# Moving the next batch's group norm and projections out of the head of a batch and in between the expert tiles of the batch before

## The chip, the cores and the metric

The kernel runs on one core of a Trainium2 chip. The metric is device time in microseconds (us) for one execution of the whole program. An engine is named by its short name: PE is TensorE (matrix products), ACT is ScalarE, DVE is VectorE, POOL is GpSimd, SP is the queue of SyncE that issues DMAs. PEld is PE's loading of weights, which runs beside its products.

## What is computed

Four images of 64 x 64 positions with 128 channels go through two layers. All is float32.

```
# layer 0, per batch: N = 4096 tokens, 4 heads of 32
xn  = group_norm(x)                       # 32 groups of 4 channels
q, k, v = split(xn @ w_qkv)
q, k = q / |q|, k / |k|                   # norm along the tokens, per channel
x = x + softmax(10 * q k^T) v @ w_out + b_out
# layer 1, linear attention
z = layer_norm(x);  q, k, v = split(W_qkv z)
q = softmax(q, over a head's 32 channels) * 32**-0.5;  k = softmax(k, over the tokens)
context = k v^T (per head);  y = W_out (context q) + b
x = x + norm_over_everything(y) * gn_w + gn_b
# layer 1, experts
z = layer_norm(x);  p = softmax(z @ router_w + router_b)
x = x + sum over the best 2 of 8 experts of weight * (z @ expert_w[e] + expert_b[e])
```

## The kernel before

The batches run one after the other (`for b in range(batches)` on each engine). The instructions of every engine are written out in program order by hand, and engines meet at semaphores (`wait_ge`, `then_inc`). No scheduler moves anything. PSUM is used as eight banks `BK[0]` to `BK[7]` of 128 x 512 float32. A "chunk" is 512 tokens (8 in a batch, `NCH`), a "tile" 128 tokens (32 in a batch, `T`).

A batch has four stages, given here with the times of the second change of batch in the trace (batch 1 to batch 2), which the prediction follows:

- **The head of a batch** (1540 to 1572 us). After the last expert tile DVE ends the group norm's factor (`s_gn`). PE transposes the batch's x, which waits in `XN` (L1127, 32 transpositions). DVE and ACT write it, scaled and shifted, into `XT` by turns. PE makes keys and queries from it (8 chunks each, `projected`) and then values (32 tiles of 128 tokens). DVE and ACT evict them and take the sums of squares and the maximum of the squares of q. DVE turns these into deviations and a flag (`s_bound`, `s_flag`), scales `Q`, and attention can start.
- **Attention** (1572 to 2117 us): 8 chunks of 32 tiles. PE makes scores, ACT exponentials, PE the products with `V`, DVE adds the exponentials up in `ACC`, which shares its memory with `XT`. SP loads the next batch's x into `XN` in this stage, and DVE takes its group statistics between the adds. At its end `projected_first` on PE multiplies chunks 0 to 6 by `WOUT0`.
- **Linear attention** (1359 to 1453 us for batch 1). DVE adds onto `X` (L915) and takes a layer norm in two halves. PE transposes z into `XT`, makes keys (`s_k1`), then values of layer 1 (`token_major(..., s_v1)`), which ACT evicts into `V` (`values1`, L577), then queries. ACT takes the exponentials of the keys (L599), PE transposes them and sums `K^T V` into `BK[0]`, DVE makes `CTX` and `AT` out of it.
- **Experts** (1464 to 1540 us). For each of the 32 tiles PE makes the products with all 8 experts into two banks (`expert_bank`, three such pairs, `EBUF = 3`; PE may be three tiles ahead). DVE multiplies four of them by the gates and adds them to `X` (L1091), ACT scales the other four (L636), POOL adds those up. `biases` and `gates` are small products of PE that come every four tiles and twice. DVE has the routing of both halves to do ahead of and between its first tiles.

The two places that matter for order: PE waits for `s_comb` and `s_zx` of the tile three before it ahead of every expert tile, and at the top of a batch for those of all tiles.

## Time and profile before

| | |
|---|---|
| median of 3 runs | 3062.41 us (3049.99 to 3062.47) |
| the profiled execution | 3062.7 us, its span 3060.9 us |
| PE busy | 2890.6 us, 94% of the span |
| DVE, ACT, POOL busy | 84%, 79%, 23% |
| mean granted clock of TensorE | 0.974 |
| attention, one chunk | 67.8 us, 8 chunks a batch |
| one batch to the next | 757.7 us |

The shares are means over stages with different limits. Time of the profiled execution outside its span is 1.8 us. A stage is read from the chain that ended last and from the timeline of its engines. Matmul records are counted as two where a float32 product takes two passes; a transposition has one.

### The profile page before, as it was taken

How to read it: one execution, taken by the hardware profiler on the slowest of the kernel's cores; microseconds unless marked ns; L12 is line 12 of the kernel's file. 1: busy time of each engine (PE TensorE's matmuls, PEld its weight loads, DVE VectorE, ACT ScalarE, POOL GpSimd, SP SyncE). 2: the span in 40 equal slices, each digit the busy share in tenths (PEclk: the TensorE clock that was granted, in tenths of full speed). 3: DMA queues.
4: the chain of work that ended last, by engine and by line, in shares of the span. 5: the costliest groups of instructions: out<-in, count | busy, mean ns of one | idle time of the engine just before them, and what ended most of it. 6: DMA issues, size and time to landing. Idle time of an engine off the chain costs nothing.

```text
span 3060.9 us, 52576 instructions
## 1 busy us (share of the span) xinstructions
PE 2890.6 (94%) x20414; PEld 1024.5 (33%) x20414; DVE 2576.4 (84%) x3687; ACT 2415.2 (79%) x3141; POOL 712.6 (23%) x726
## 2 busy tenths in 40 slices
PE   6999999989899999998989999999898999999988
PEld 3222222275422222237532222223743222222474
DVE  6888888878788888986878888898687888888867
ACT  5999999753799999974479999997447999999734
POOL 1122222113312222111432222121152222121115
PEclk9999999998999999999899999999899999999989
DMA  2655555500265555550026555554002555555300
GB/s 88 115 111 111 109 113 111 98 1 14 59 121 109 111 112 111 97 97 1 21 66 116 113 112 111 99 111 84 1 21 56 112 112 113 101 109 110 73 1 28
DMA packets 72081, 257.03 MB, mean 84 GB/s; under 512 B 8160, under 2 KB 10240, under 8 KB 71808
## 3 DMA queue, kind: packets, MB, share of 16 engines
q0 software_dynamic: 64512, 234.91, 40.6%
q1 hardware_dynamic: 7296, 18.51, 1.6%
q8 instruction: 168, 2.75, 0.4%
q14 instruction: 105, 0.86, 0.1%
HBM read 10.12 MB, written 8.39 MB: 6 GB/s over the span
## 4 chain that ended last, share of the span: by engine, by line
PE 84%; DVE 8%; ACT 5%; issue 2%; POOL 1%; DMA 0%; SPq 0%; POOLq 0%; DVEq 0%; ACTq 0%
PE BK L1122 81%; PE BK L1127 3%; DVE X L1091 2%; ACT EA L548 2%; ACT KE L548 2%; DVE MXS L941 1%; DVE ST L668 1%; ACT K L599 1%; POOL KE L473 1%; ACT SMC L537 0%; DVE KE L700 0%; DVE XT L824 0%; DVE RU L662 0%; DVE RU L661 0%; PE BK L1424 0%
## 5 line engine op out<-in xcount | busy, mean ns | idle before, releaser
L877 DVE TENSOR_TENSOR XT<-XT,KE 128x512 f32<-128x512 f32 x1344 | 1572.7, 1226 | 148.8 <-ACT KE L548 146.4
L548 ACT ACTIVATE KE<-BK 128x512 f32<-128x512 f32 (+1 forms) x1536 | 1490.5, 1022 | 129.9 <-PE BK L1122 34.5
L1122 PE MATMUL BK<-Q,K 32*128 32x512 f32 x8192 | 1167.8, 640 | 18.5 <-ACT KE L548 12.2
L1122 PE MATMUL BK<-KE,V 128*32 128x512 f32 x6144 | 815.0, 604 | 5.3 <-ACT SMC L537 5.3
L432 POOL DMA_DIRECT2D RM<-EA x448 | 393.3, 959 | 1506.9 <-ACT EA L548 650.3
L1122 PEld LDWEIGHTS BK<-Q,K 32*128 32x128 f32 x8192 | 319.9, 183 | 874.8 <-ACT KE L548 626.6
L548 ACT ACTIVATE EA<-BK 128x512 f32<-128x512 f32 (+1 forms) x512 | 497.5, 1025 | 26.6
L1122 PEld LDWEIGHTS BK<-KE,V 128*32 128x32 f32 x6144 | 125.3, 108 | 582.7 <-issue 533.0
L1122 PE MATMUL BK<-EA,V 128*32 128x512 f32 x2048 | 272.6, 604 | 0.0
L636 ACT ACTIVATE RM<-BK,GT 128x128 f32<-128x128 f32 x512 | 146.3, 368 | 139.6 <-PE BK L1122 139.6
L1122 PE MATMUL BK<-WEXP,XT 128*128 128x512 f32 x512 | 243.0, 621 | 14.0 <-DVE X L1091 14.0
L1091 DVE SCALAR_TENSOR_TENSOR X<-BK,GT,X 128x128 f32<-128x128 f32 x512 | 175.1, 350 | 32.5 <-PE BK L1122 16.3
L851 DVE TENSOR_TENSOR XT<-KE 128x512 f32<-128x512 f32 x64 | 88.8, 1393 | 124.2 <-ACT KE L548 124.2
L482 POOL TENSOR_TENSOR Z<-RM 128x512 f32<-128x512 f32 x64 | 81.2, 1269 | 272.2 <-ACT RM L636 272.2
L1122 PEld LDWEIGHTS BK<-WEXP,XT 128*128 128x128 f32 x512 | 98.1, 201 | 124.3 <-issue 93.5
L413 POOL TENSOR_TENSOR Q<-PVC,REC 128x512 f32<-128x512 f32 x32 | 70.1, 2189 | 250.5 <-DMA RM<-EA 125.4
L1122 PEld LDWEIGHTS BK<-EA,V 128*32 128x32 f32 x2048 | 40.7, 108 | 193.5 <-issue 171.1
L831 DVE RECIPROCAL REC<-SMC 128x512 f32<-128x512 f32 x28 | 93.6, 3342 | 0.0
L1122 PE MATMUL BK<-WQKV,XT 128*128 128x128 f32 x768 | 89.4, 276 | 0.0
L1122 PEld LDWEIGHTS BK<-WQKV,XT 128*128 128x128 f32 x768 | 87.9, 192 | 4.0 <-issue 3.8
L1122 PE MATMUL BK<-XT,WQKV 128*128 128x512 f32 x192 | 86.5, 604 | 0.0
L824 DVE TENSOR_TENSOR XT<-XT,RM 128x512 f32<-128x512 f32 x64 | 75.3, 1217 | 0.2 <-POOLq L440 0.2
(182 smaller groups left out, 1849.3 us busy)
## 6 DMA issues: line engine op xcount, KB each, us to landing
RM<-EA POOLq DMA_DIRECT2D x224, 768.0 KB, 6.7
RM<-EA POOLq DMA_DIRECT2D x224, 256.0 KB, 3.3
XN<-in_x SPq DMA_DIRECT2D x16, 512.0 KB, 6.2
out<-X SPq DMA_DIRECT2D x16, 512.0 KB, 2.6
WEXP<-in_L_ffn_expert_w SPq DMA_DIRECT2D x1, 512.0 KB, 6.6
CONST<-in_consts SPq DMA_DIRECT2D x1, 384.0 KB, 5.4
WQKV<-in_L_conv_w_qkv SPq DMA_DIRECT2D x1, 192.0 KB, 2.2
WQKV<-in_L_attn_W_qkv SPq DMA_DIRECT2D x1, 192.0 KB, 5.8
```

What stands on the lines that cost most here:

```text
L413: nc.gpsimd.tensor_tensor(Q[:, c * CH:(c + 1) * CH], PVC[:, :], REC[:, :], ALU.mult).then_inc(s_ot, 1)
L432: nc.gpsimd.dma_start(DACC[:, PART[p]], EA[:, k % 2, PART[p]], accum_op=ALU.add).then_inc(s_dacc[p], 16)
L482: nc.gpsimd.tensor_tensor(Z2[:, :, :], z[:, :, 0:2 * C], z[:, :, 2 * C:4 * C], ALU.add).then_inc(s_zs, 1)
L548: nc.scalar.activation(exps(jt, p), scored(c * T + jt, p).rearrange("p a n -> p (a n)"), ACT.Exp, scale=SCALE0).then_inc(s_exp, 1)
L636: last = nc.scalar.activation(ZX[:, t // 2 % 2, t % 2, k], expert_bank(t, 1)[:, k], ACT.Copy, scale=GT[:, t, e:e + 1])
L824: v.tensor_tensor(acc, acc, DACC[:, PART[p]], ALU.add).then_inc(s_merge, 1)
L831: v.reciprocal(REC[:, :], row_sums).then_inc(s_rec, 1)
L851: v.tensor_tensor(ACC[:, par, PART[p]], exps(0, p), exps(2, p), ALU.add).then_inc(s_adds, 1)
L877: v.tensor_tensor(acc, acc, exps(jt, p), ALU.add).then_inc(s_adds, 1)
L1091: v.scalar_tensor_tensor(X[:, t, :], expert_bank(t, 0)[:, e * C:(e + 1) * C], GT[:, t, e:e + 1], X[:, t, :], ALU.mult, ALU.add).then_inc(s ...
L1122: return nc.tensor.matmul(o, lhsT, rhs, start=start, stop=stop, skip_group_check=shared)
L1127: last = nc.tensor.transpose(dst[:, (t % TPB) * P:(t % TPB + 1) * P], src(t), IDENT)
```

## The change

What it does:

- `V` is free between attention and the next batch's attention, since layer 1 has no values of its own any more: PE sums `K^T z` (`Z` holds z as tokens) and multiplies the 128 x 128 result by the value weights once (`KZ`, `s_kz`). `values1`, its 32 records on PE for each half and its 8 evictions on ACT are gone.
- After the last products of attention, PE transposes the next batch's x (`turned_following`, 32 transpositions into banks 4, 5 and 6 by turns), and ACT copies it raw into `V` (`VT`, `s_raw`). The `WOUT0` products of chunks 4 to 6 go behind the first half's transpositions of z.
- The group norm's two small products and its chain of DVE operations go to the middle of layer 1 (`group_means`, `group_moments`, `group_spread`, `group_norm`), and ACT normalises `VT` in place in two lots of four chunks (`normalise`).
- The 24 projections of the next batch (8 keys, 8 queries, 8 chunks of values) stand behind 24 of the 32 expert tiles (`project_following`, all but every fourth tile), in banks 5 and 6. ACT evicts them alone (`evicted`), with the squares. Expert tiles have two pairs of banks (three in the last batch).
- DVE takes the maxima of q's squares after the tiles of chunks 5 and 6, the deviations ahead of chunk 7, the flag among chunk 7's tiles.
- Batch 0 has its head as before.

On PE, the expert stage of batch 0. `BK<-WEXP,XT` is an expert tile (two instructions), `BK<-EB,GTT` the biases, `G` and `GTT` the gates, `V` the next batch's x. Before, from the first expert tile:

```order
L1122 MATMUL BK<-WEXP,XT 128x512 x2
L1424 MATMUL BK<-CONST,G 128x128 x4
L1122 MATMUL BK<-WEXP,XT 128x512 x2
L1122 MATMUL BK<-EB,GTT 128x128 x4
L1122 MATMUL BK<-WEXP,XT 128x512 x4
L1122 MATMUL BK<-EB,GTT 128x128 x4
L1122 MATMUL BK<-WEXP,XT 128x512 x8
```

In the changed kernel, from the same place:

```order
L1218 MATMUL BK<-WEXP,XT 128x512 x2
L1552 MATMUL BK<-CONST,G 128x128 x4
L1218 MATMUL BK<-WEXP,XT 128x512 x2
L1218 MATMUL BK<-V,WQKV 128x512
L1218 MATMUL BK<-EB,GTT 128x128 x4
L1218 MATMUL BK<-WEXP,XT 128x512 x2
L1218 MATMUL BK<-V,WQKV 128x512
L1218 MATMUL BK<-WEXP,XT 128x512 x2
L1218 MATMUL BK<-V,WQKV 128x512
L1218 MATMUL BK<-EB,GTT 128x128 x4
L1218 MATMUL BK<-WEXP,XT 128x512 x4
L1218 MATMUL BK<-V,WQKV 128x512
```

A projection now stands behind three of each four tiles, so PE is nowhere idle by order, and the transpositions and products of the head of the next batch are gone.

On DVE, the end of the same stage. `X<-BK8,GT,X` is a gated add of one expert, `MXS` the maxima, `Q` the queries. Before:

```order
L1083 TENSOR_TENSOR X<-BK8,X 128x512
L1091 SCALAR_TENSOR_TENSOR X<-BK8,GT,X 128x128 x16
L1083 TENSOR_TENSOR X<-BK8,X 128x512
L1091 SCALAR_TENSOR_TENSOR X<-BK8,GT,X 128x128 x16
```

In the changed kernel, from the maxima after chunk 6 on (the chain for the deviations is 15 rows, of which the first and last stand here):

```order
L805 TENSOR_REDUCE MXS<-KE 128x1 x4
L810 TENSOR_REDUCE RA<-MXS 128x1
...
L816 TENSOR_TENSOR SMALL<-SMALL,RA 128x1
L828 TENSOR_SCALAR Q<-Q,SMALL 128x512
L1160 TENSOR_TENSOR X<-BK8,X 128x512
L1171 SCALAR_TENSOR_TENSOR X<-BK8,GT,X 128x128 x8
L821 TENSOR_REDUCE SMALL<-BK8 1x1
```

Between the last add of tile 27 and the first of tile 28 DVE now has four maxima, the chain and one scaling.

On PE, behind attention. `WOUT0,Q` are the output products of layer 0, `XT,CONST` the sums of the last chunk, `XN` the next batch's x, `KE` z, `WQKV1` the weights of layer 1. Before:

```order
L1122 MATMUL BK8<-WOUT0,Q 128x128 x16
L1122 MATMUL BK8<-XT,CONST 32x512 x4
L1122 MATMUL BK8<-WOUT0,Q 128x128 x12
L1300 UNCONDITIONAL_BRANCH
L1127 MATMUL BK8<-CONST,KE 128x128 x16
L1122 MATMUL BK8<-XT,WQKV1 128x512 x4
L1122 MATMUL BK8<-WOUT0,Q 128x128 x4
L1122 MATMUL BK8<-WQKV1,XT 128x128 x32
```

In the changed kernel:

```order
L1218 MATMUL BK8<-WOUT0,Q 128x128 x16
L1223 MATMUL BK8<-CONST,XN 128x128 x8
L1218 MATMUL BK8<-XT,CONST 32x512 x4
L1223 MATMUL BK8<-CONST,XN 128x128 x24
L1416 UNCONDITIONAL_BRANCH
L1223 MATMUL BK8<-CONST,KE 128x128 x16
L1218 MATMUL BK8<-WOUT0,Q 128x128 x12
L1218 MATMUL BK8<-XT,WQKV1 128x512 x4
L1218 MATMUL BK8<-WOUT0,Q 128x128 x4
L1218 MATMUL BK8<-WQKV1,XT 128x128 x16
```

The transpositions of x took the place of twelve `WOUT0` products, which moved behind z's transpositions, ahead of the keys and of chunk 7's `WOUT0` products; 16 products of layer 1's values are gone.

The diff, cut to its core:

```diff
 def group_bank(b):
-            return BK[0] if b else BK[NCH - 1]
+            return BK[5] if b else BK[NCH - 1]
+        def expert_buffers(b):
+            return 2 if b + 1 < batches else 3
+        def projection_of(t):
+            return t - 1 - t // TPB if t % TPB else None
+        def projection_bank(j):
+            return BK[5 + j % 2]
+        def turned_bank(i):
+            return BK[HCH + i % 3]
...
# ACT, behind attention
+                if b + 1 < batches:
+                    for i in range(NCH):
+                        act.wait_ge(s_xT, (b + 1) * NCH + i + 1)
+                        nc.scalar.activation(VT[:, i * CH:(i + 1) * CH], turned_bank(i), ACT.Copy).then_inc(s_raw, 1)
...
# ACT, layer 1 and experts
-                for c in range(HCH, NCH):
-                    values1(c)
...
+                def normalise(chunks):
+                    act.wait_ge(s_gn, b + 2)
+                    for c in chunks:
+                        xt = VT[:, c * CH:(c + 1) * CH]
+                        nc.scalar.activation(xt, xt, ACT.Identity, bias=SMALL[:, 4:5], scale=SMALL[:, 3:4]).then_inc(s_xn, 1)
+                def evicted(j):
+                    c, columns = j % NCH, slice(j % NCH * CH, (j % NCH + 1) * CH)
+                    act.wait_ge(s_proj, (b + 1) * (3 * NCH) + j + 1)
+                    if j < NCH:
+                        nc.scalar.activation(SQ[:, 0, columns], projection_bank(j), ACT.Square, accum_out=SS[:, 0, c:c + 1])
+                        nc.scalar.activation(K[:, columns], projection_bank(j), ACT.Copy).then_inc(s_kev, 1)
...
+                    if following and t and projection_of(t - 1) is not None:
+                        evicted(projection_of(t - 1))
...
# DVE
+                dve.wait_ge(s_ctx, b * 3 + 1)
+                v.tensor_copy(KZ[:, :], BK[0][:, 0:C]).then_inc(s_kz, 1)
+                dve.wait_ge(s_ctx, b * 3 + 2)
+                v.scalar_tensor_tensor(CTX[:, :], BK[0][:, C:2 * C], SMALL[:, 11:12], BLOCK,
                                        ALU.mult, ALU.mult).then_inc(s_at, 1)
...
+                if following:
+                    pre_link, pre_n = chain(s_pre, (b + 1) * PRE_LINKS)
+                    group_spread(b + 1)
+                    group_norm(b + 1, pre_link)
...
# PE, experts
+                def project_following(j):
+                    m, c = j // NCH, j % NCH
+                    if j >= 2:
+                        before = j - 2
+                        signal = (s_kev, s_qev, s_v)[before // NCH]
+                        pe.wait_ge(signal, (b + (signal is s_v)) * NCH + before % NCH + 1)
+                    if m == 0:
+                        pe.wait_ge(s_xn, b * NCH + c + 1)
...
+                    if following and t == T - 2:
+                        pe.wait_ge(s_bound, b + 2)
                         pe.wait_ge(s_eba, b * NCH + HCH)
+                        mm(bound_bank(b + 1)[0:1, 0:H], SMALL[:, 14:15], BLOCK[:, 0:P:D]).then_inc(s_gm, 1)
+                    if t >= buffers:
+                        pe.wait_ge(s_comb, b * COMB + (t - buffers + 1) * NDVE)
+                        pe.wait_ge(s_zx, b * T + t - buffers + 1)
...
+                    if following and projection_of(t) is not None:
+                        project_following(projection_of(t))
```

## Rows read from the trace of the kernel before

**Rows 1.** The page: busy time of an engine; chain's shares.

```profile
PE 2890.6 (94%) x20414; PEld 1024.5 (33%) x20414; DVE 2576.4 (84%) x3687; ACT 2415.2 (79%) x3141; POOL 712.6 (23%) x726
...
PE 84%; DVE 8%; ACT 5%; issue 2%; POOL 1%; DMA 0%; SPq 0%; POOLq 0%; DVEq 0%; ACTq 0%
```

**Rows 2.** The chain that ended last, whole program: start, length, work.

```profile
1396.51 4.08 ACT K L599 x4
...
1544.08 5.19 PE BK L1127 x32
```

**Rows 3.** Timeline of PE, last expert tiles and first scores: start, length, work, [idle before].

```profile
1531.65 7.11 PE L1122 MATMUL BK<-WEXP,XT 128*128 128x512 f32 x16
...
1572.18 1.14 PE L1122 MATMUL BK<-Q,K 32*128 32x512 f32 x8 [0.78 <-ACT V L519]
```

**Rows 4.** Groups by line and shape, 1540.3 to 1572.2 us: busy, mean ns.

```profile
L1122 PE MATMUL BK<-XT,WQKV 128*128 128x512 f32 x32 | 13.9, 592 | 0.0
L1122 PE MATMUL BK<-WQKV,XT 128*128 128x128 f32 x64 | 7.6, 277 | 0.0
```

**Rows 5.** Timeline of PE in the expert stage.

```profile
1473.60 1.98 PE L1122 MATMUL BK<-WEXP,XT 128*128 128x512 f32 x4 [0.61 <-DVE X L1091]
...
1499.78 1.12 PE L1424 MATMUL BK<-CONST,G 128*128 128x128 f32 x4 [2.64 <-DVE GT L1072]
1500.68 6.37 PE L1122 MATMUL BK<-WEXP,XT 128*128 128x512 f32 x12
...
1507.79 7.03 PE L1122 MATMUL BK<-WEXP,XT 128*128 128x512 f32 x16
```

**Rows 6.** Windows: length, busy of PE, PEld, DVE, ACT, POOL; clock, DMA, GB/s.

```profile
1463.90:1538.80 74.90, 68.73 (x207) 34.51 (x207) 61.88 (x178) 35.63 (x125) 40.28 (x44) 0.95 0.05 22
1373.00:1377.00 4.00, 4.00 (x18) 3.69 (x19) 4.00 (x5) 4.00 (x10) 0.00 (x0) 0.57 0.00 0
1545.00:1549.00 4.00, 4.00 (x29) 4.00 (x28) 2.56 (x4) 2.12 (x3) 0.00 (x0) 0.73 0.04 12
```

**Rows 7.** Timeline of ACT: an expert tile, then evictions of a query chunk.

```profile
1538.81 1.14 ACT L636 ACTIVATE RM<-BK,GT 128x128 f32<-128x128 f32 x4 [0.51 <-PE BK L1122]
...
1558.39 0.58 ACT L513 ACTIVATE KE<-BK 128x512 f32<-128x512 f32 x1
...
1558.96 0.59 ACT L516 ACTIVATE Q<-BK 128x512 f32<-128x512 f32 x1
```

**Rows 8.** Timeline of DVE: first expert tiles, then maxima and deviations.

```profile
1471.31 0.69 DVE L1083 TENSOR_TENSOR X<-BK,X 128x512 f32<-128x512 f32 x1 [2.05 <-PE BK L1122]
1472.04 5.76 DVE L1091 SCALAR_TENSOR_TENSOR X<-BK,GT,X 128x128 f32<-128x128 f32 x16
...
1564.73 1.28 DVE L767 TENSOR_REDUCE MXS<-KE 128x1 f32<-128x512 f32 x2 [0.20 <-ACT KE L513]
1566.05 0.16 DVE L780 TENSOR_REDUCE RA<-MXS 128x1 f32<-128x8 f32 x1
...
1569.05 0.48 DVE L788 TENSOR_SCALAR Q<-Q,SMALL 128x512 f32<-128x512 f32 x1
```

**Rows 9.** Timelines of linear attention, batch 1, one engine after the other.

```profile
1365.11 2.94 PE L1122 MATMUL BK<-WOUT,Q 128*128 128x128 f32 x24
1372.92 3.54 PE L1127 MATMUL BK<-CONST,KE 128*128 128x128 f32 x16 [4.87 <-DVE KE L700]
...
1401.22 6.62 PE L1127 MATMUL BK<-CONST,K 128*128 128x128 f32 x32 [3.53 <-ACT V L577]
...
1380.91 0.69 DVE L915 TENSOR_TENSOR X<-BK,X 128x512 f32<-128x512 f32 x1 [0.47 <-PE BK L1122]
...
1418.67 0.35 DVE L976 SCALAR_TENSOR_TENSOR CTX<-BK,SMALL,CONST 128x128 f32<-128x128 f32 x1 [3.42 <-PE BK L1122]
```

**Rows 10.** Timelines of POOL and DVE at the start of attention.

```profile
1570.81 10.65 POOL L405 TENSOR_TENSOR X<-XN,BO 128x1024 f32<-128x1024 f32 x4 [27.85 <-DVE FLAG L793]
...
1577.85 5.22 DVE L851 TENSOR_TENSOR XT<-KE 128x512 f32<-128x512 f32 x2 [6.01 <-ACT KE L548]
```

340 lines of the change are left out of this document (203 added, 137 removed).

## The prediction

> **What bounds the kernel now.** I read the page first. PE is busy for 94% of the span and the chain that ended last lies on it for 84% [rows 1]. Then the chain in order of time: attention is one pattern of PE pieces, 67.8 us a chunk, which the change leaves as it is, and the head of a batch, which starts on PE at 1544.1 us for batch 2 [rows 2], comes back every 757.7 us, so one change of batch stands for three. There are four batches and so three such changes, and one last batch without a successor. Within one change I read three timelines: expert tiles to the first scores (rows 3 to 8), linear attention (rows 9), and the start of attention (rows 10).
>
> PE's last expert tile ends at about 1538.8 us and its first scores start at 1572.2 us [rows 3]. These 33.4 us are what the change wants to be rid of. In the expert stage ahead, 74.9 us long, PE is busy 68.7 and waits 6.2 us, DVE is busy 61.9, ACT only 35.6 us [rows 6]. So ACT has room there and PE has not: what is put between the tiles lengthens the stage on PE.
>
> **The change part by part.**
>
> *The head, -30.6 us each.* The 33.4 us go. In their place, after the last tile: ACT starts on it about 0.2 us after PE, copies for 1.14 us [rows 7], and evicts two chunks of values at about 0.6 us each, the time of the copy in [rows 7]; some 0.3 us are handovers and the reading of the flag, which fits into the 0.78 us that PE now waits for the same eviction [rows 3]. That is 2.8 us. DVE scales seven chunks of Q meanwhile, which only the second chunk of attention needs.
>
> *The expert stage, +23.3 us each.* The keys and queries took 32 records in 13.9 us, the values 64 in 7.6 us [rows 4]. 23 of the 24 projections stand ahead of the last tile: 13.9 + 7/8 x 7.6 = 20.5 us. The three small products of the group norm leave the stage, -0.4 us. The rest is PE's waits, 6.2 us before. With two pairs of banks a tile waits for the one two before it. A tile takes PE 7.03 / 4 = 1.72 us of issue once it is warm [rows 5], a projection 0.87, so four tiles with three projections and a product of biases (0.9) take 10.4 us. DVE needs 4 x 1.44 + 0.7 = 6.5 us for them [rows 8], ACT 4 x 1.14 for copies and three evictions of 0.57 + 0.59 [rows 7], 8.0 us. So PE sets the pace wherever DVE has nothing else. Following the tiles with these durations, PE waits in these places: tile 2 for DVE's tile 0, whose biases come a projection later, 2.4 us; 1.1 and 0.7 us behind the routing operations that DVE has between its chunks; 1.3 us for the second gates, where it waited 2.64 us before [rows 5], as PE arrives later; 0.4 and 0.2 us at two more tiles; and at tile 30. There DVE has put four maxima (4 x 0.61 = 2.5 us), the chain to the deviations (1566.05 to 1569.05, 3.0 us) and one scaling (0.4 us) ahead of tile 28 [rows 8], and tile 30 needs the banks of tile 28. From the end of tile 27: DVE 1.65 to its own end, 5.9, biases 0.65, tile 28 1.45, handover 0.1, in all 9.7 us; PE has 6.4 us of work until then, so it waits 3.3 us. Sum of waits 9.4 us. The stage grows by 20.5 - 0.4 + 9.4 - 6.2 = 23.3 us.
>
> *Linear attention, +2.3 us each.* Behind attention PE has a gap of 4.87 us [rows 9]. The x transpositions (32 in 5.2 us in [rows 2]) fit into it with the 2.9 us of products that leave it: PE ends at about 1369, ACT's copies at 1369.5, and z is not there before 1372. So they cost nothing; without that cover they would cost up to their 5.2 us. But the 24 records of WOUT0 (2.9 us) now stand ahead of the keys and of chunk 7's product, for which DVE already waits, at 1380.91 [rows 9]. From there DVE's chain to the exponentials of the keys comes 2.8 us later. The values of layer 1 give back almost as much: the transpositions of the keys at 1401.22 waited for ACT's eviction of a value [rows 9], though the first of the two halves of exponentials (4.08 us from 1396.51) was done at 1398.6 [rows 2]. Without it PE starts 2.6 us earlier. I add 0.3 for a clock that is low once more while z is transposed, net +0.5. The 64 records of PE are otherwise covered by DVE's chain. Then CTX: it follows the sum at once, at 1418.67 [rows 9]; now a copy, eight transpositions of PE that stand ahead (0.95 us) and one more product come between, +1.3 us, and the row sums for which POOL waits stand behind it. The group's moments stand ahead of the second output product, +0.5; the group norm's DVE chain (some 16 steps of 0.2 us) pushes the statistics by 1.2 us, but PE has route products until after DVE's next result. The two lots of normalisation on ACT (8 x 0.8 us) lie in gaps of 8 and 11 us.
>
> *The start of attention, 0.* POOL's first bias sum no longer waits for a flag but for the stores of X; DVE waits for POOL. POOL's 10.65 us [rows 10] start about 4 us after the first scores where they started 1.4 us before them. DVE's first two adds took 5.2 us beside POOL [rows 10], and more adds will now stand beside it. I expect DVE 3 to 4 us later. Exponentials stand in a ring of six with about eight tiles (16 us) of slack, and DVE, busy 84% of the span [rows 1], catches up within a chunk, so this is hidden. If it were not, it would cost those 4 us.
>
> *The last batch, -1.2 us.* It has no x to transpose, keeps three pairs of banks, gains the 2.5 us at the keys' transpositions and pays 1.3 at CTX.
>
> Sum of one change of batch: -30.6 + 23.3 + 2.3 = -5.0 us. Against the profiled execution, 3062.7 us with the 1.8 us around its span: 3062.7 - 3 x 5.0 - 1.2 = **3046.5 us**. The profiled execution stands 0.3 us over the median of the runs, 3062.4; one of the three runs was 3050.0. A measurement of this kernel can tell about 0.5% (15 us) from no change.
>
> Bounds of the uncertain terms, each per change of batch. Expert stage: without any wait +13.9 us. On the other side, a low clock after each long wait: after the wait of 2.64 us twelve records took 6.37 us where sixteen take 7.03 later [rows 5], 1.1 us more, twice 2.2; and 2.4 us for the loop in the third rival, together 27.9. Linear attention: +0.3, if the shorter gap leaves the clock up for z's transpositions; +5.2, if it also stays low for the WOUT0 products. I stay near the middle in both, since rows 5 show waits of that length with and without such a loss.
>
> **The rule that speaks against it.** The clock granted was 0.57 for 1373 to 1377 us, after the gap, that is the lower level of 1.2 GHz for most of it, and 0.73 in 1545 to 1549 us, while 32 transpositions of x ran [rows 6]. In the changed kernel transpositions are the last thing ahead of the gap, and the WOUT0 products come behind it. The Trainium skill, page "TensorE: Matmul & The Clock Gate", section "Part 4: PE-mode transpose", says that a transposition doesn't count as work of PE the way a product does, so that full clock is not reached by it. By that rule the clock would stay low through the WOUT0 products. The trace agrees only in part, since the clock rose while x was transposed.
>
> **Rivals.**
> 1. *The waits are absorbed.* DVE has 3.9 us of slack in four tiles. If the waits at tiles 2, 13 and 30 are short and the clock stays up between the denser products, the stage grows by 15 to 19 us. With +17 and +1 in linear attention: 3 x (-12.6) - 1.2, 3024 us; range 3012 to 3040.
> 2. *The clock at the low level behind the gap.* If the x transpositions leave the clock low and the 24 records of WOUT0 run at half speed, DVE gets chunk 7 another 2.9 us later; with the 2.2 us of slow tiles after the long waits that makes 5.1 us more a change of batch: 3062 us, no change. Range 3053 to 3070. The rule above would give 2.9 us of it, 3055 us alone.
> 3. *The eviction loop on ACT sets the pace, slower than before.* A projection waits until ACT has evicted the one two before it, and that eviction stands behind the copies of the next tile. The loop over two tiles is: projection 0.87, tile 1.72, handover 0.25, copies 1.14, eviction 1.16, handover 0.1, 5.2 us, and PE's own time for two tiles is also 5.2. So it decides from here on: every 0.1 us in it is paid at each of 8 pairs of key and query tiles. It costs 0.3 us a loop (2.4 us) if ACT's reading of the sum of squares isn't hidden. If handovers added 1.5 to 2 us a loop, or PE could not run ahead at all and waited 0.6 us at each of 24 tiles, the stage would grow by 14 us more: 3046.5 + 43 = 3089 us. For it: the margin is nothing. Against: ACT runs copies back to back in this stage and idles 0.51 us ahead of each tile [rows 7].
> 4. *x is not hidden.* If ACT's copies and PE's transpositions went in turn (1.25 us a chunk, three banks), eight would end at 1375, 3 us late: 3055 us.
>
> **How the numbers follow.** Forecast (3040 to 3053): 0.43. Rival 1: 0.22. Rival 2 with rival 4: 0.25. Rival 3 as slower: 0.10. The range runs from inside rival 1 (0.06 of it left out below) to the upper end of rival 2 and leaves out rival 3: 3020 to 3070 us, 0.84 within. Faster by over 0.5% is below 3047.1: all of rival 1 and somewhat over half of the forecast's, 0.24, so 0.46. Slower by over 0.5% is above 3077.7: 0.10. Within: 0.44.
>
> **What would show it.** The first scores of batch 2 should start near 1567 us less the earlier gain, so that one batch to the next takes 752.7 us instead of 757.7. The stage from the first expert tile to the last should be about 98 us long, PE busy about 89 of it, with a wait on DVE of 3 us ahead of tile 30 and of 2.4 us ahead of tile 2. From the last tile to the first scores there should be 3 us. The last product of WOUT0 should be near 1383.5, CTX 1.8 us later than before from the same start. ACT's idle time ahead of its copies should be gone in the tiles with keys and queries. The forecast is wrong if PE waits for ACT at the projections, if PE's clock in the expert stage is below 0.9, or if attention's first chunk is longer than before.

## The result

The changed kernel takes 3069.84 us (median of 18 runs, 3068.14 to 3071.25), the kernel before 3062.45 us in the runs beside it (18 runs, 3049.99 to 3065.22). The ratio is 1.0034 with a 95% interval of 1.0024 to 1.0043. By the medians it is 7 us slower, by the ratio 10, where 16 us less had been forecast. The two differ because the kernel before spreads: its runs lie near 3050, 3054 and 3061 to 3065 us, with granted clocks of 0.983, 0.980 and 0.974; those of the changed kernel lie within 3 us. The result is within 0.5% of no change and, by 0.2 us, inside the wide range, but it is on the other side of zero from the forecast and outside the forecast's own range of 3040 to 3053 us. The profiled execution took 3069.15 us. In the series below one run of all_four (8943.55 us), one of head_early (10694.44 us) and one of the kernel before beside head_early (5094.48 us) were in a slow state and are left out of the ratios.

The page of the changed kernel, its busy times and the engines' shares of the chain that ended last, against [rows 1]:

```profile
PE 2885.4 (94%) x20166; PEld 994.5 (32%) x20166; DVE 2551.1 (83%) x3643; ACT 2428.6 (79%) x3181; POOL 711.0 (23%) x726
...
PE 83%; DVE 9%; ACT 5%; issue 2%; POOL 1%; DMA 0%; SPq 0%; POOLq 0%; DVEq 0%; ACTq 0%
```

PE is 5 us less busy in a span that is 6.4 us longer. The mean granted clock fell from 0.974 to 0.966. The page can't say more than that. The stages can, each measured between the same two events in PE's timeline (first product of `WOUT0`, start of the first and end of the last expert tile, first scores). The times are those from batch 1 to the first scores of batch 2, and of batch 2's attention, in us:

| | before | after | difference | forecast |
|---|---|---|---|---|
| head: last expert tile to first scores | 33.4 | 2.95 | -30.5 | -30.6 |
| expert tiles, first to last | 74.8 | 103.0 | +28.2 | +23.3 |
| linear attention, `WOUT0` to first expert tile | 104.9 | 104.5 | -0.4 | +2.3 |
| attention, first scores to `WOUT0` | 544.5 | 550.7 | **+6.2** | 0 |
| sum of one change of batch | | | +3.5 | -5.0 |
| last batch | | | -4.4 | -1.2 |

Three times 3.5 less 4.4 is 6.1 us, against the 6.4 us between the two spans. Without the line in bold, three times 6.2 us, the changed kernel would have taken some 3050 us: an estimate from these rows.

**Expert stage and head.** PE's timeline in the changed kernel: start, length, work, [idle before it and what ended that].

```profile
1478.18 2.80 PE L1218 MATMUL BK<-WEXP,XT 128*128 128x512 f32 x4 [2.33 <-DVE X L1171]
1480.77 1.92 PE L1218 MATMUL BK<-V,WQKV 128*128 128x512 f32 x2
...
1484.27 1.02 PE L1218 MATMUL BK<-V,WQKV 128*128 128x512 f32 x2
...
1561.72 0.19 PE L1218 MATMUL BK<-CONST,SMALL 128*1 128x4 f32 x2 [2.50 <-DVE SMALL L816]
1564.26 3.54 PE L1218 MATMUL BK<-WEXP,XT 128*128 128x512 f32 x4 [2.35 <-DVE X L1171]
...
1573.49 1.14 PE L1218 MATMUL BK<-Q,K 32*128 32x512 f32 x8 [2.05 <-ACT V L660]
1575.35 2.09 PE L1218 MATMUL BK<-Q,K 32*128 32x512 f32 x8 [0.72 <-ACT KE L574]
1578.19 2.09 PE L1218 MATMUL BK<-Q,K 32*128 32x512 f32 x8 [0.75 <-ACT EA L574]
```

Windows of the expert stage and of 20 us around the first scores: length, busy time of PE, PEld, DVE, ACT and POOL, granted clock, DMA share, GB/s.

```profile
1467.57:1570.55 102.98, 91.21 (x293) 46.67 (x294) 74.65 (x214) 55.07 (x179) 40.82 (x45) 0.94 0.04 16
1572.00:1592.00 20.00, 14.79 (x64) 3.65 (x64) 9.29 (x6) 12.34 (x14) 13.91 (x7) 0.57 0.16 51
```

The second of these in the kernel before, where the first scores start at nearly the same time [rows 3]:

```profile
1572.00:1592.00 20.00, 16.10 (x124) 4.01 (x124) 14.15 (x10) 18.14 (x21) 11.25 (x6) 1.00 0.49 143
```

The second window holds most of the loss. In the kernel before the clock is at its full level (granted 1.00, 2.4 GHz) and a score tile (8 records, 1.14 us) comes every 1.89 us. In the changed kernel the granted clock is 0.57, the lower level of 1.2 GHz for most of the 20 us. The clock falls just behind the wait: the first score tile still takes 1.14 us, each of the next five takes 2.09 us, and they come every 2.84 us. PE gets through 64 records instead of 124. It was idle for 2.50 and 2.35 us around tile 30 and for 2.05 us ahead of the first scores. Tile 30 behind the first two waits took 3.54 us instead of 1.88; the next tile took 1.88 us again.

**DVE ahead of tile 30**, timeline of the changed kernel:

```profile
1554.58 2.45 DVE L805 TENSOR_REDUCE MXS<-KE 128x1 f32<-128x512 f32 x4
...
1559.73 1.14 DVE L814 TENSOR_TENSOR SMALL<-SMALL 128x1 f32<-128x1 f32 x1
...
1560.97 0.70 DVE L816 TENSOR_TENSOR SMALL<-SMALL,RA 128x1 f32<-128x1 f32 x1
1561.59 0.47 DVE L828 TENSOR_SCALAR Q<-Q,SMALL 128x512 f32<-128x512 f32 x1
```

**Start of the attention**, DVE and POOL in the changed kernel, against [rows 10]:

```profile
1585.66 4.99 DVE L916 TENSOR_TENSOR XT<-KE 128x512 f32<-128x512 f32 x2 [10.71 <-ACT KE L574]
...
1579.32 9.72 POOL L430 TENSOR_TENSOR X<-XN,BO 128x1024 f32<-128x1024 f32 x4 [2.91 <-DMA out<-X]
```

POOL's four bias additions start 5.8 us after the first scores where they started 1.4 us ahead of them, because they wait for the store of the last quarter of x. POOL's first accumulation (`RM<-EA`, which adds exponentials by a DMA) starts 20.0 us after the first scores instead of 13.8. DVE's first addition starts 12.2 us after the first scores instead of 5.7.

**Linear attention**, PE and then DVE in the changed kernel, against [rows 2, 9]:

```profile
1369.54 2.99 PE L1223 MATMUL BK<-CONST,XN 128*128 128x128 f32 x24
1377.36 3.34 PE L1223 MATMUL BK<-CONST,KE 128*128 128x128 f32 x16 [4.84 <-DVE KE L750]
1380.54 2.84 PE L1218 MATMUL BK<-WOUT,Q 128*128 128x128 f32 x24
...
1463.02 4.70 PE L1218 MATMUL BK<-WR,XT 128*128 128x8 f32 x32 [0.69 <-ACT XT L587]
...
1387.75 0.69 DVE L980 TENSOR_TENSOR X<-BK,X 128x512 f32<-128x512 f32 x1 [2.38 <-PE BK L1218]
...
1423.71 0.35 DVE L1043 SCALAR_TENSOR_TENSOR CTX<-BK,SMALL,CONST 128x128 f32<-128x128 f32 x1 [0.74 <-PE BK L1218]
```

The x transpositions are hidden, DVE waits 2.38 us for chunk 7 as the prediction had it, and `CTX` comes 0.9 us later than before from the same start (60.6 against 59.7 us after `WOUT0` began; forecast 1.8). The router products of the second half took 4.70 us; in the kernel before they took 6.99:

```profile
1457.07 6.99 PE L1122 MATMUL BK<-WR,XT 128*128 128x8 f32 x32 [0.69 <-ACT XT L557]
```

The granted clock was 0.78 in them (1463.02 to 1467.57 us) and 0.50 in the kernel before (1457.07 to 1463.90 us). These 2.3 us are the clock's, and the prediction's sum has no term for them.

### The profile page after: what moved, and what is told of

Read it like the earlier page. It is cut to its first block, busy times and chain, and to the rows that moved or that the text cites. A ratio compares the mean times of both kernels' runs of the same rounds, so it can differ in the third digit from the quotient of the medians.

```text
span 3067.3 us, 52091 instructions
## 1 busy us (share of the span) xinstructions
PE 2885.4 (94%) x20166; PEld 994.5 (32%) x20166; DVE 2551.1 (83%) x3643; ACT 2428.6 (79%) x3181; POOL 711.0 (23%) x726
## 4 chain that ended last, share of the span: by engine, by line
PE 83%; DVE 9%; ACT 5%; issue 2%; POOL 1%; DMA 0%; SPq 0%; POOLq 0%; DVEq 0%; ACTq 0%
PE BK L1218 81%; PE BK L1223 2%; ACT EA L574 2%; DVE X L1171 2%; ACT KE L574 2%; DVE ST L718 1%; DVE MXS L1006 0%; ACT SMC L563 0%; DVE X L1160 0%; POOL KE L498 0%; DVE KE L750 0%; DVE MXS L805 0%; DVE XT L889 0%; ACT K L621 0%; DVE X L980 0%
## 5 line engine op out<-in xcount | busy, mean ns | idle before, releaser
L1218 PE MATMUL BK<-Q,K 32*128 32x512 f32 x8192 | 1183.8, 648 | 22.3 <-ACT KE L574 12.2
L1218 PE MATMUL BK<-WEXP,XT 128*128 128x512 f32 x512 | 253.1, 630 | 26.1 <-DVE X L1171 26.1
L1223 PE MATMUL BK<-CONST,KE 128*128 128x128 f32 x256 | 50.4, 363 | 40.5 <-DVE KE L750 32.6
L927 DVE TENSOR_TENSOR RM<-EA,KE 128x512 f32<-128x512 f32 x64 | 75.3, 1217 | 0.0
L498 POOL TENSOR_TENSOR KE<-KE,QSUM 128x512 f32<-128x512 f32 x32 | 32.9, 1049 | 150.1 <-DVE QSUM L1024 150.1
```

The lines of the kernel that those rows point to most:

```text
L927: v.tensor_tensor(DACC[:, PART[p]], exps(1, p), exps(3, p), ALU.add).then_inc(s_adds, 1)
L1218: return nc.tensor.matmul(o, lhsT, rhs, start=start, stop=stop, skip_group_check=shared)
L1223: last = nc.tensor.transpose(dst[:, (t % TPB) * P:(t % TPB + 1) * P], src(t), IDENT)
```

## The experiments

Three questions were open. Is the low clock the cause of the longer attention, and which wait brings it about? Is the late start of DVE and POOL a second cause? Do the rest of the terms add up as the table says? All kernels but two (before_gap and before_kz) start from the changed kernel. Products of PE whose result nobody reads are called idle products. The stages are those of each kernel's one profiled execution, in us: attention of batches 1 to 3 as a range, the others as the mean of batches 0 to 2. The ratio is to the kernel before in runs of the same series.

| kernel | attention | linear attention | expert tiles | head | median, us | ratio to before, 95% |
|---|---|---|---|---|---|---|
| the kernel before | 544.5 | 104.8 | 74.8 | 33.4 | 3062.45 | |
| the changed kernel | 550.7 | 104.5 | 103.1 | 2.96 | 3069.84 | 1.0034 [1.0024, 1.0043] |
| fill_head | 547.3 to 550.1 | 103.9 | 102.9 | 3.40 | 3063.22 | 1.0003 [0.9993, 1.0013] |
| fill_wait30 | 548.5 to 549.6 | 104.2 | 101.4 | 2.99 | 3059.11 | 0.9996 [0.9985, 1.0007] |
| before_gap | 550.5 to 550.6 | 104.7 | 74.0 | 35.3 | 3083.04 | 1.0068 [1.0051, 1.0086] |
| before_kz | 544.5 | 101.2 | 74.6 | 33.8 | 3049.78 | 0.9966 [0.9945, 0.9987] |
| bias_late | 558.4 to 565.5 | 103.7 | 102.9 | 2.96 | 3117.81 | 1.0190 [1.0163, 1.0217] |
| head_and_bias | 551.9 to 558.7 | 104.0 | 103.1 | 3.40 | 3100.12 | 1.0133 [1.0106, 1.0159] |
| spread | 549.4 to 553.1 | 104.0 | 98.1 | 2.97 | 3057.24 | 0.9995 [0.9980, 1.0011] |
| all_four | 555.8 to 558.4 | 103.5 | 96.4 | 3.40 | 3081.93 | 1.0069 [1.0044, 1.0094] |
| zs_wait | 550.5 to 554.9 | 104.4 | 103.1 | 2.96 | 3072.99 | 1.0056 [1.0033, 1.0079] |
| head_zs | 548.1 to 552.4 | 104.1 | 103.1 | 3.40 | 3070.81 | 1.0042 [1.0027, 1.0057] |
| spread_head_zs | 547.9 to 551.7 | 104.5 | 96.5 | 3.40 | 3050.40 | 0.9970 [0.9958, 0.9983] |
| early | 550.6 to 550.7 | 104.4 | 103.0 | 2.96 | 3069.21 | 1.0030 [1.0019, 1.0041] |
| head_early | **544.5 to 544.6** | 103.8 | 102.9 | 3.40 | 3052.61 | 0.9977 [0.9962, 0.9993] |
| spread_head_early | **544.5 to 544.6** | 103.8 | 96.4 | 3.40 | **3031.22** | 0.9901 [0.9883, 0.9919] |

### Work for PE in its waits: fill_head and fill_wait30

fill_head puts three idle products of 128 x 512 behind the last projection:

```
                     if following and projection_of(t) is not None:
                         project_following(projection_of(t))
+                    if following and t == T - 1:
+                        for _ in range(3):
+                            mm(BK[7], IDENT, WEXP[:, 0:NDVE, :].rearrange("p e c -> p (e c)"))
```

> The changed kernel, with three more 128x512 products of PE (2.6 us, their result is used by nobody) behind the last projection, ahead of the first scores of batches 1 to 3. Theory A (the clock is low in the first 18 us of attention because PE is idle for 2.05 us just ahead of the first scores, and scores at 60% duty can't raise it): the first scores come 0.5 us later, but a score tile at the start takes 1.9 us again instead of 2.84, each of three attentions is 6.2 us shorter, so 3069.8 - 3 x 5.7 = 3053 us. Theory B (the clock is low because of the long waits around expert tile 30, and it would be low with or without that gap): the three products only cost, 3071 us, the clock in the 18 us stays at 0.57.

fill_wait30 does the same with five, ahead of the wait for the deviations at tile 30:

```
                     if following and t == T - 2:
-                        pe.wait_ge(s_bound, b + 2)
                         pe.wait_ge(s_eba, b * NCH + HCH)
+                        for _ in range(5):
+                            mm(BK[0], IDENT, WEXP[:, 0:NDVE, :].rearrange("p e c -> p (e c)"))
+                        pe.wait_ge(s_bound, b + 2)
```

> The changed kernel, with five more 128x512 products of PE (4.3 us, result used by nobody) ahead of the wait for the bound at expert tile 30, where PE waited 4.85 us for DVE. Theory A: tile 30 takes 1.8 us instead of 3.54, 1.9 us saved at each of three places, the start of attention stays at the low clock, 3069.8 - 5.7 = 3064 us. Theory B: the start of attention is at the full clock too, 3069.8 - 3 x 8.1 = 3045.5 us.

PE's timeline in fill_head, first scores of batch 2, and ACT's at tile 13 of batch 1:

```profile
1567.79 2.74 PE L1218 MATMUL BK<-WEXP,CONST 128*128 128x512 f32 x6
...
1572.35 1.14 PE L1218 MATMUL BK<-Q,K 32*128 32x512 f32 x8 [0.75 <-ACT KE L574]
...
841.71 1.94 ACT L574 ACTIVATE EA<-BK 128x512 f32<-128x512 f32 x2 [2.26 <-POOLq L465]
```

PE's timeline in fill_wait30:

```profile
1568.35 1.14 PE L1218 MATMUL BK<-Q,K 32*128 32x512 f32 x8 [2.14 <-ACT V L660]
1570.21 1.14 PE L1218 MATMUL BK<-Q,K 32*128 32x512 f32 x8 [0.72 <-ACT KE L574]
...
1599.35 1.14 PE L1218 MATMUL BK<-Q,K 32*128 32x512 f32 x8 [2.51 <-ACT EA L574]
```

In both the granted clock is 1.00 in the first score tiles of all three attentions, with idle products in either of the two places. With the wait at tile 30 filled, PE still idles 2.14 us ahead of the first scores and keeps its full clock, so a wait of that length there doesn't by itself lower it. But only 0.6 to 3.4 of the 6.2 us came back, and no expected time was met (fill_head 3063 us instead of 3053 or 3071, fill_wait30 3059 instead of 3064 or 3045.5). ACT, which never waited for POOL in the attention of the changed kernel, now waits 1.6 to 4.4 us in all for POOL to hand a slot of exponentials back (2.26 us at tile 13 in the row above), and PE waits for ACT. A second loss lies behind the first.

### The low clock in the kernel before: before_gap

In the kernel before, for batches 1 to 3, one more copy on ACT (into `DACC`, which is unused then) stands ahead of the last eviction of values and makes PE wait there:

```
                     act.wait_ge(s_proj, b * (3 * NCH) + 2 * NCH + c + 1)
+                    if b and c == NCH - 1:
+                        act.wait_ge(s_zs, b * PAIRS)
+                        nc.scalar.activation(DACC[:, :], K[:, 0:4 * CH], ACT.Copy)
```

> The kernel before, with one more copy on ACT (128x2048, 1.9 us, its result is used by nobody) ahead of the last eviction of layer 0's values in batches 1 to 3, so that PE waits 2.7 us instead of 0.78 ahead of the first scores. Theory A: the wait and the low clock, 3 x (1.9 + 6.2) = 24 us longer, 3086.5 us, clock in the first 18 us of attention near 0.6. Theory B: the wait alone, 3 x 1.9 = 5.7 us longer, 3068 us, clock 1.00.

PE's timeline at the first scores of batch 2:

```profile
1583.17 1.14 PE L1125 MATMUL BK<-Q,K 32*128 32x512 f32 x8 [2.58 <-ACT V L522]
1585.04 2.09 PE L1125 MATMUL BK<-Q,K 32*128 32x512 f32 x8 [0.72 <-ACT KE L551]
```

The head is 1.8 us longer and the attention 6.1 us, with nothing changed in its program or in POOL's, and the granted clock in its first 20 us is 0.57. ACT doesn't wait for POOL here. So a longer wait of PE ahead of the first scores is enough for the whole loss: 1.8 us more of waiting cost 6.1 us in the attention behind it, 3.4 times as much. Theory A had 3086.5 us, measured were 3083.0.

### Layer 1 without its values, alone: before_kz

The kernel before with `values1` taken out and the sum over keys and z with the product `KZ` behind it, as in the changed kernel; all else as before:

```
-                        token_major(c, WQKV1[:, 2 * C:3 * C], s_v1)
...
-                    last = mm(BK[0][:, 0:C], KT[:, t * P:(t + 1) * P], V[:, t, :], start=(t == 0), stop=(t == T - 1))
+                    last = mm(BK[0][:, 0:C], Z[:, t * C:(t + 1) * C], KT[:, t * P:(t + 1) * P], start=(t == 0), stop=(t == T - 1))
...
+                    if i == 2:
+                        pe.wait_ge(s_kz, b + 1)
+                        mm(BK[0][:, C:2 * C], KZ[:, :], WQKV1[:, 2 * C:3 * C]).then_inc(s_ctx, 1)
```

> The kernel before, with one part of the change alone: no values in layer 1, the keys' product with z is multiplied by the value weights once. By the prediction's sum 1.2 us less a batch, 4.8 in all, 3057.6 us. By the last batch of the changed kernel's trace, which has this part alone and took 4.4 us less than before, up to 17.6 us less in four batches, 3045 us. If the order without values costs as much as it gives, 3062 us.

PE's timeline: transpositions of the keys, and the router products of the second half.

```profile
1396.67 5.38 PE L1126 MATMUL BK<-CONST,K 128*128 128x128 f32 x32 [3.92 <-ACT K L598]
...
1452.44 4.44 PE L1121 MATMUL BK<-WR,XT 128*128 128x8 f32 x32 [0.69 <-ACT XT L559]
```

This part alone is worth 10 us by the ratio and 13 by the medians. But single runs of the kernel before came out at 3050 us too, so part of it may be a clock that the kernel before is granted in some of its runs; no trace of such a run is kept. In the two traces linear attention is 3.6 us shorter: `CTX` comes 1.2 us earlier after `WOUT0` began, the 1.2 us that the prediction had for this part, and the router products of the second half run 2.5 us faster, 4.44 instead of 6.99 us. Why the clock is higher there stays open.

### The chain of deviations in pieces: spread

DVE's maxima, the chain to the deviations and the first scaling are spread in pieces of at most about 1 us, one behind each of tiles 18 to 24 and up to four behind each of tiles 25 to 27, instead of standing ahead of tile 28 in one:

```
-                    if following and c == NCH - 3:
-                        for q in range(HCH):
-                            q_maximum(b + 1, q)
...
+                    for t in range(c * TPB, (c + 1) * TPB):
+                        combined(range(t, t + 1))
+                        if t == 18 or 19 <= t < 25:
+                            next(left, None)
+                        elif t >= 25:
+                            for _ in range(4):
+                                next(left, None)
```

> The changed kernel, with DVE's maxima and the chain of the deviations cut into pieces of at most 1 us that stand behind one expert tile each (tiles 18 to 27), so that PE does not wait 4.85 us around tile 30. Theory A (the clock falls through the waits of PE, this one and the 2 us ahead of the first scores together): the expert stage is 6 us shorter (the wait and the slow tile 30), and attention starts at the full clock, as it did when that wait was filled with products, 3 us more: 3069.8 - 3 x 9 = 3043 us. If only the wait goes and the clock stays low at the start of attention: 3069.8 - 3 x 6 = 3052 us.

PE's timeline:

```profile
1549.58 1.98 PE L1249 MATMUL BK<-WEXP,XT 128*128 128x512 f32 x4 [0.86 <-DVE X L1171]
...
1553.40 1.98 PE L1249 MATMUL BK<-WEXP,XT 128*128 128x512 f32 x4 [0.82 <-DVE X L1171]
...
1565.10 2.09 PE L1249 MATMUL BK<-Q,K 32*128 32x512 f32 x8 [0.73 <-ACT EA L574]
...
2315.15 1.14 PE L1249 MATMUL BK<-Q,K 32*128 32x512 f32 x8 [2.05 <-ACT V L660]
2317.01 1.14 PE L1249 MATMUL BK<-Q,K 32*128 32x512 f32 x8 [0.72 <-ACT KE L574]
```

And ACT's, in the attention of batch 3:

```profile
2344.25 1.94 ACT L574 ACTIVATE EA<-BK 128x512 f32<-128x512 f32 x2 [1.18 <-POOLq L465]
```

The waits of 2.50 and 2.35 us became 0.86 and 0.82, the slow tile is gone, and the stage is 4.9 us shorter. The clock of the first scores is lost all the same in batches 1 and 2 (granted 0.66 over 20 us), behind waits of 2.11 and 2.06 us. In batch 3 of the same execution it is kept (1.00) behind 2.05 us, and fill_wait30 had kept it behind 2.14. So neither that wait nor those at tile 30 decide alone; what does is not to be had from these runs. In every kernel without the wait ahead of the scores the clock was kept.

This one execution also shows the two losses apart. Where the clock was lost, the attention took 549.4 us and ACT never waited for POOL. Where it was kept, ACT waited 5.2 us in all for POOL, and the attention took 553.1 us.

### POOL's additions: bias_late, head_and_bias, all_four

bias_late moves POOL's four bias additions behind its second to fifth accumulation of the first chunk, and DVE waits for POOL's last pair addition (`s_zs`) instead of the first bias addition:

```
                             accumulate(c, k)
+                            if c == 0 and 2 <= k < 6:
+                                biased_x(k - 2)
```

> The changed kernel, with POOL's four additions of the output bias onto x moved from ahead of attention to behind its second to fifth accumulation in the first chunk, and DVE waiting for POOL's last expert sum instead of for the first of these additions. Theory C (there are two delays at the start of attention: PE's low clock, and DVE and POOL, which start 6 us later than before because of the additions; in the changed kernel the first hides the second): with the clock still low nothing is gained beyond 1 us at each of three places, 3067 to 3070 us. Theory D (DVE's late start is what makes attention 6.2 us longer): 3069.8 - 3 x 6 = 3052 us.

head_and_bias has the idle products of fill_head too; all_four has those, spread, and two more idle products at expert tile 2.

> Both: three more products of PE ahead of the first scores, and POOL's additions later. With the products alone attention took 548.1, 547.3 and 550.1 us where the kernel before takes 544.5, and ACT waited 2 us for POOL's accumulation in the first chunk. Theory C: attention is back at 544.5 to 545 us, 11 us less in all than with the products alone, 3052 us. Rival: the rest of the loss is something else (the order of the additions does not matter), 3062 us.

> The changed kernel with DVE's pieces spread, three more products ahead of the first scores, two more ahead of expert tile 2 (where PE waits 2.3 us and two tiles then run slowly), and POOL's additions later. By the terms measured so far, each change of batch: 6 us less in the expert stage, 2 at tile 2, 6.2 in attention, 0.5 more ahead of the scores: 3069.8 - 3 x 13.7 = 3029 us. Rival: DVE becomes the bound of the expert stage once PE no longer waits at tile 30, the stage shrinks by less than 4 us: 3040 us.

POOL and ACT of bias_late in the first chunk of batch 0:

```profile
106.37 7.17 POOL L429 TENSOR_TENSOR X<-XN,BO 128x1024 f32<-128x1024 f32 x1 [6.33 <-DMA RM<-EA]
...
137.03 1.94 ACT L577 ACTIVATE EA<-BK 128x512 f32<-128x512 f32 x2 [5.97 <-POOLq L464]
```

POOL, busy 23% of the span, has no room there. It waits some 6 us for its own transfer in each round, ACT hands it new work every 8.3 us, and the slot is handed back only behind the transfer. An addition of 2.4 to 7.2 us in each of four rounds makes ACT wait for slots, 5 to 11 us in all. The attention took 551.9 to 565.5 us in these three kernels, 7 to 21 more than the 544.5 of the kernel before, and 557.0 to 559.0 in batch 0, where the kernel before takes 544.8. All expectations were missed (all_four took 3082 us, with 3029 or 3040 expected). These runs leave the first two questions open; what they show is that POOL can't be given this work in the loop without making ACT wait.

### DVE earlier, POOL as it is: zs_wait and head_zs

```
-                dve.wait_ge(s_bias, b * 4 + 1)
+                dve.wait_ge(s_zs, b * PAIRS)
```

> The changed kernel with one wait exchanged: VectorE's wait for the first of GpSimd's four bias additions, ahead of the attention, becomes a wait for the last of GpSimd's pair additions of the batch before; GpSimd's own order stays. TensorE's wait ahead of the first scores stays too. Theory A (two losses one behind the other; the clock's hides the late VectorE's): VectorE's first addition of exponentials starts some 7 us behind the first scores instead of 12.2, but the score tiles still come every 2.1 us at about half clock for 18 us; the attention stays at 549 to 551 us, the kernel at 3066 to 3071 us. Theory B (the late VectorE keeps TensorE waiting and so its clock low): with VectorE early the clock is back after the first tiles, the attention takes 545 to 547 us, the kernel 3053 to 3060 us.

> The kernel of fill_head (three idle products ahead of the first scores) with the same exchange of VectorE's wait. Theory A: the full clock is there at the first tile, VectorE's first addition starts 7 us behind the first scores instead of 11 to 12, GpSimd's first accumulation about 4 us earlier, and ScalarE's wait of 2.3 us for GpSimd at tile 13 is gone; the attention takes 544.5 to 545.5 us instead of 547.3 to 550.1, the kernel 3050 to 3056 us. Rival (the rest of the loss in fill_head is from GpSimd alone, whose additions run 9.8 us beside the first tiles and start 5 us later than before the change): VectorE is earlier but its additions there take 1.8 us and more each beside GpSimd, the wait at tile 13 stays, the attention stays above 547 us and the kernel at 3061 to 3065 us.

DVE, POOL and ACT of head_zs behind the first scores, which start at 2340.23 us:

```profile
2347.24 5.55 DVE L916 TENSOR_TENSOR XT<-KE 128x512 f32<-128x512 f32 x2 [6.01 <-ACT KE L574]
2352.72 6.70 DVE L927 TENSOR_TENSOR RM<-EA,KE 128x512 f32<-128x512 f32 x2
...
2346.06 11.75 POOL L430 TENSOR_TENSOR X<-XN,BO 128x1024 f32<-128x1024 f32 x4 [3.37 <-DMA out<-X]
...
2368.15 1.94 ACT L574 ACTIVATE EA<-BK 128x512 f32<-128x512 f32 x2 [0.68 <-POOLq L465]
```

The rival of head_zs holds, and the kernel is slower still than it said. DVE starts 7.0 us after the first scores as wanted, but its first four additions take 12.3 us (5.55 + 6.70) instead of 7.3 (4.99 + 2.35), and POOL's 11.8 instead of 9.7: side by side both are slower, until POOL is done. POOL's first accumulation starts 19.8 us after the first scores, where it started 19.7 in fill_head. The attention gets no shorter: head_zs is 0.4% slower than fill_head by their ratios (1.0042 against 1.0003), and zs_wait, at 3073 us, no faster than the changed kernel. In zs_wait DVE is early and the granted clock is 0.57 all the same, so DVE's late start isn't what lowers the clock. DVE's wait in the changed kernel cost nothing.

spread_head_zs has spread, the idle products of fill_head, two more at expert tile 2, and the exchanged wait.

> All three mends in one, with GpSimd's order left as it is: VectorE's maxima and deviations in pieces of at most 1 us behind the tiles 18 to 27 (spread), three idle products ahead of the first scores, two at expert tile 2, and the exchanged wait. Theory A, the terms add up: expert tiles 96.5 us instead of 103.0, attention 544.5 to 545.5 instead of 550.7, head 3.4 instead of 2.95; per change of batch 6.5 + 5.7 - 0.45 = 11.75 us, three times, so 3034 to 3037 us, faster than the kernel before by 0.8 to 0.9 per cent. Rival (the wait at tile 13 stays, as in head_zs's rival): attention 547 to 550, the kernel 3043 to 3050 us.

The expert tiles came out as expected, 96.5 us, and the attention as in its rival or worse, 547.9 to 551.7 us, so the kernel took 3050.4 us. ACT waits 2.4 to 4.8 us for POOL in each of its three attentions.

### POOL earlier: early and head_early

POOL does two quarters of the next batch's bias additions ahead of its last pair addition, where it idled 5.4 us, and each of the other two waits for its own stored quarter of x. DVE's wait is that of zs_wait. head_early has the idle products of fill_head as well.

```
-                if b:
-                    for i in range(4):
-                        pool.wait_ge(s_x_out[i], b * 16)
-                    settle(pool)
+                for i in range(2 if b else 0, 4):
+                    biased_x(b, i)
...
+                    if i == T // 2 - 1 and b + 1 < batches:
+                        for q in range(2):
+                            biased_x(b + 1, q)
```

> The changed kernel with GpSimd's and VectorE's part of head_early alone, without the idle products: TensorE's wait of about 2.1 us ahead of the first scores stays. Theory C (the low clock costs by itself: 8 or 9 score tiles at 2.84 us instead of 1.89): the attention still takes 549 to 551 us, the kernel 3066 to 3071 us. Rival (with VectorE and GpSimd early the clock comes back sooner): 545 to 547 us and 3053 to 3060 us.

> The kernel of head_zs (idle products ahead of the first scores, VectorE's exchanged wait), and GpSimd does two of its four bias additions ahead of its last pair addition, the other two each behind its own stored quarter of x instead of behind all four. Theory G (what is left of the attention's loss once the clock is kept is GpSimd's: its additions begin 5.8 us behind the first scores and run for 11.8 beside VectorE's first four additions, in the kernel before they begin 1.4 us ahead): VectorE's first four additions take 2.1 to 2.4 us per two beyond the first pair, GpSimd's first accumulation starts 13 to 14 us behind the first scores as in the kernel before (13.8) instead of 19.8, ScalarE's wait at tile 13 is gone, the attention takes 544.5 to 546 us instead of 551.6, the kernel 3050 to 3056 us. Rival (the loss comes from the idle products or from the exponentials themselves, and the additions are only beside it): the wait at tile 13 or one like it at a later tile stays, the attention is above 548 us, the kernel 3062 to 3070 us.

POOL and DVE of head_early; the first scores start at 1566.94 us:

```profile
1559.51 4.67 POOL L428 TENSOR_TENSOR X<-XN,BO 128x1024 f32<-128x1024 f32 x2
...
1569.49 2.36 POOL L428 TENSOR_TENSOR X<-XN,BO 128x1024 f32<-128x1024 f32 x1
1572.67 2.37 POOL L428 TENSOR_TENSOR X<-XN,BO 128x1024 f32<-128x1024 f32 x1 [0.82 <-DMA out<-X]
1580.14 1.91 POOL L458 DMA_DIRECT2D RM<-EA  x2 [5.10 <-DVE XT L946]
...
1573.96 3.29 DVE L920 TENSOR_TENSOR XT<-KE 128x512 f32<-128x512 f32 x2 [6.00 <-ACT KE L578]
1577.18 2.35 DVE L931 TENSOR_TENSOR RM<-EA,KE 128x512 f32<-128x512 f32 x2
```

PE of early at its first scores:

```profile
1572.39 1.14 PE L1222 MATMUL BK<-Q,K 32*128 32x512 f32 x8 [2.06 <-ACT V L664]
1574.25 2.09 PE L1222 MATMUL BK<-Q,K 32*128 32x512 f32 x8 [0.72 <-ACT KE L578]
```

With the clock kept and POOL early the attention takes 544.5 us in all three batches, that of the kernel before to a tenth. POOL's first accumulation starts 13.2 us after the first scores (19.8 in head_zs, 13.8 before), and ACT never waits for POOL. With POOL early and the clock low (early) the attention takes 550.6 us. Both came out as theories G and C had it. So there are two losses, 6.1 us by the clock and 3 to 8 us by POOL (fill_head, head_zs), which run side by side: taking away one uncovers the other, and taking away POOL's alone gives nothing.

### All mends together: spread_head_early

spread, the idle products of fill_head, two more at tile 2, and POOL's and DVE's part of early.

> All mends together: spread, the idle products ahead of the first scores and at expert tile 2, the exchanged wait and GpSimd's early additions. Theory G, the terms add up: expert tiles 96.5 to 97 us, head 3.4, attention 544.5 to 546, linear attention 103.5 to 104.5; per change of batch 105.0 + 96.5 + 3.4 + 545.3 = 750 us against the 757.7 of the kernel before, so 3 times 7.5 less and 2 to 4 for the last batch: 3034 to 3040 us, faster by 0.7 to 0.9 per cent. Rival of head_early: attention above 548, 3045 to 3052 us.

```profile
span 3029.5 us, 52163 instructions
...
PE 2865.2 (95%) x20196; PEld 988.1 (33%) x20196; DVE 2546.8 (84%) x3643; ACT 2427.1 (80%) x3181; POOL 707.4 (23%) x726
```

The terms add up: one batch to the next takes 747.8 to 748.9 us against the 757.5 to 757.8 of the kernel before, and the kernel 3031.2 us, a little less than the 3034 to 3040 expected. It is 1.0% faster than the kernel before (ratio 0.9901, 0.9883 to 0.9919). So the change did have a gain in it, some 31 us by the medians, of which 10 to 13 are those of before_kz. The changed kernel lost it in the waits of the expert stage and at the start of the attention.

## Why the prediction was wrong

**The start of the attention, 0: the step that failed.** The prediction saw POOL's additions move from 1.4 us ahead of the first scores to 4 us behind (5.8 measured) and DVE become 3 to 4 us late (6.5 measured), and called both hidden, since the exponentials have a ring with 16 us of slack and DVE catches up. DVE did. In the changed kernel the term was wrong by 6.2 us, and what makes these up is PE's clock: before_gap shows 6.1 us for it in an attention that is otherwise that of the kernel before. The prediction never asked for the clock here, though it had itself put a wait of 3.3 us at tile 30 and a shortened handover ahead of the scores: rival 2 looked for the low clock behind the gap of linear attention, and behind the waits in the expert stage, and priced it by the records next to the wait. The sentence that attention is "one pattern of PE pieces" which the change "leaves as it is" is where the search stopped too early: the pattern is left as it is, but not the level of the clock that it runs at behind the new waits. The prediction also left out POOL, which waits for DVE's fourth addition before its first accumulation and hands ACT's slots back in a loop that has no slack (bias_late, head_zs). Those 3 to 8 us are hidden in the changed kernel and show only once the clock is kept. One of the prediction's own signs of being wrong, a first chunk of attention longer than before, is the one that came.

**The expert stage, +23.3: the mechanism was right, the size was not** (+28.2, just above the upper bound of 27.9). PE was busy 91.2 us of the stage (forecast about 89). The waits came where they were expected, at tile 2 (2.33 us, forecast 2.4), behind routing (1.28 and 1.23, forecast 1.1 and 0.7), at the second gates (1.73, forecast 1.3), and sum to 11.8 us instead of 9.4. More than half of that excess is at tile 30: 2.50 and 2.35 us, 4.85 in all, instead of 3.3, since two operations on one number each took 1.14 and 0.70 us beside POOL instead of the 0.16 of such a step [rows 8]. The rest of the stage's excess, 2.4 us, is PE's own work at the lower clock level: tile 2 took 2.80 us and tile 30 3.54, where a tile takes 1.88 at full clock. The prediction had worked it out as 2.2 us, and kept it for its bounds. spread and fill_wait30 confirm the place at tile 30, with a stage 4.9 and 1.7 us shorter. Rival 3, ACT's loop, did not come: no wait of PE for ACT stands between the tiles.

**The head, -30.6: right** to 0.1 us. The 2.8 us behind the last tile were there, and so was the wait of 2.05 us in them that turned out to matter.

**Linear attention, +2.3, and the last batch, -1.2: the mechanisms held, and a clock was missing.** x fits into the gap, so rival 4 fell; the `WOUT0` products cost what they should. The router products start 2.4 us (first half) and 1.9 us (second half) later after `WOUT0` began than before, near the 2.3. The second half's then gave back 2.3 us by a higher clock, which puts the stage at -0.4 us, below the lower bound of +0.3. In the last batch, without the `WOUT0` and x part, the same gain stands alone, 3.9 of its 4.4 us.

**The rule weighed.** After the gap z's 16 transpositions took 3.34 us, where the 24 of x ahead of it took 2.99, and the 24 records of `WOUT0` right behind them 2.84 us: the granted clock was 0.54 in the transpositions (1377.36 to 1380.50 us) and 1.00 in the products (1380.54 to 1383.20 us). By the Trainium skill, "TensorE: Matmul & The Clock Gate", "Part 4: PE-mode transpose", transpositions don't bring the full clock; as the prediction applied it, the products should have been slow. The trace doesn't agree, and the price of 3055 us that the prediction gave for this rule alone didn't come.

**The chances.** Slower by over 0.5% had 0.10 and did not come; no measurable change had 0.44 and did. That the result lies inside the wide range, 3020 to 3070 us, is luck: the five terms were off by 0.1 us (head), -2.7 (linear attention), +4.9 (expert stage), +6.2 (start of the attention) and -3.2 us (last batch), partly against each other. The largest of these misses was in the term that had been given a single value and no bound above 4 us.

**A slip in its working.** A tile's 1.72 us is written as 7.03 / 4, which is 1.76; 1.72 us is what a tile takes from its start to that of the next piece (1494.44 to 1496.16 us in the changed kernel), so the sum stands.

## What to carry to other kernels

When a change takes a stretch of dense PE work away from ahead of a loop that waits on another engine at every step, ask whether PE's waits just ahead of the loop lower its clock there: here waits of 2 to 2.5 us, which would have cost their own length, cost 6 us more in the tiles behind them, and three idle products ahead of the loop kept the clock. Then look at who hands buffers back in that loop, and in what phase: an engine that is busy 23% of the time can have no slack at all, and work that shifts by 6 to 7 us against the loop shows up only after the larger loss beside it is gone. When one mend brings nothing back, the loss that it aims at isn't refuted: run the mends together before dropping either.
